# Silu on ScalarE in the shared MLP of a Mamba and mixture-of-experts layer

## What is computed

```python
xn = layernorm(x)
# mamba branch with a shared MLP behind it
h  = xn + mamba_mixer(rmsnorm(xn), ...)
s  = h + silu(rmsnorm(h) @ mlp_w1.T) @ mlp_w2.T      # 256 -> 1024 -> 256
# mixture of 8 experts, the 2 best of each token
g  = silu(moe(xn, ...))
out = x + s * g

def mamba_mixer(x, ...):                # 512 inner channels, 16 states
    xp, z = split(x @ in_proj_w.T)
    xc = silu(conv4(xp))
    dt = softplus(...); B, C = ...      # from xc @ x_proj_w.T
    state = state * exp(dt * A) + dt * xc * B        # a scan over the tokens
    y = sum_over_states(state * C) + xc * D
    return (y * silu(z)) @ out_proj_w.T
```

## The kernel before

| event | step in the period | what |
|---|---|---|
| A.IN0 to IN3, CV, TH, SL0 to SL3 | +15 to +39 | conv input, its taps on VectorE (L1395), tanh on ScalarE (L855), silu's multiplication on VectorE (L1405) |
| C.M100, M101, M102, M103 | +28, +31, +33, +35 | first MLP product for the first 256 tokens of the block, two of the eight 128-row groups in each |
| C.YE0, YE1 | +38 | the sum over states is taken in (L1420) |
| A.XD | +40 | x_proj on TensorE (L997, prod<-xc,par) |
| C.M200, M201 | +38, +40 | second MLP product of these tokens |
| C.Z0 | +41 | product for the gate z, tanh (L889), two multiplications on VectorE (L1426, L1434) |
| C.M110 to M113 | +43, +45, +47, +50 | first MLP product for the other 256 tokens |
| A.DT0 to DT3 | +44 to +50 | dt, Abs and Relu on ScalarE (L868, L869) |
| A.SPE, SPL | +51, +52 | softplus: Exp (L874), then Ln (L882); ScalarE comes to them 2 steps later by LATER |
| C.M210, M211, STORE | +53, +55, +57 | second MLP product, the block's result to DRAM (SP) |
| C.RMS, NORM | +17, +18 | Square (L894), Sqrt (L897), the norm's scaling (L901) |

## Time and profile before

### The profile page before, as it was taken

How to read it: one execution, slowest core, us unless ns; L and a number is a source line. 1 busy time by engine, 2 the same in 40 slices (tenths; PEclk the granted TensorE clock), 3 DMA queues, 4 the chain that set the end, 5 groups by cost and what they waited for, 6 DMA issues and landing times.

```text
span 1574.1 us, 17157 instructions
## 1 busy us (share of the span) xinstructions
PE 1273.4 (81%) x4966; PEld 922.0 (59%) x4966; DVE 1301.1 (83%) x1571; ACT 886.1 (56%) x1948; POOL 1197.2 (76%) x626
## 2 busy tenths in 40 slices
PE   3874563988979988988878997999978898889977
PEld 2641121765667747766756766775766576646546
DVE  6699875698879987999988986998889897977834
ACT  4642352584757656575757665775747374545532
POOL 0544888786898869887997779887988789896840
PEclk8586886899999979999989998999999998979989
DMA  4774443775496728685676748784868559455640
GB/s 165 263 268 146 161 147 106 267 256 175 144 317 208 244 89 268 232 259 164 201 250 231 221 145 274 227 246 148 256 224 251 181 172 302 140 191 188 211 152 27
DMA packets 129790, 319.50 MB, mean 203 GB/s; under 512 B 14984, under 2 KB 29712, under 8 KB 119200
## 3 DMA queue, kind: packets, MB, share of 16 engines
q1 hardware_dynamic: 112224, 272.91, 50.8%
q0 software_dynamic: 11328, 35.66, 9.5%
q10 hardware_dynamic: 6144, 9.83, 1.8%
HBM read 259.75 MB, written 39.71 MB: 190 GB/s over the span
## 4 chain that ended last, share of the span: by engine, by line
PE 28%; issue 22%; POOL 21%; DVE 11%; DMA 5%; ACT 4%; SPq 1%; DVEq 0%; ACTq 0%; POOLq 0%
PE prod L997 23%; POOL hxc L737 8%; DVE state L1382 7%; POOL dbu L726 7%; DMA xs<-slot_x 4%; POOL slot_x L713 3%; PE prod L1049 1%; PE prod L1184 1%; PE prod L1002 1%; PE prod L1185 1%; DVE hxc L1350 1%; ACT state L804 1%; POOL hxc L743 1%; DVE prod L1426 1%; DVE late L1452 1%
## 5 line engine op out<-in xcount | busy, mean ns | idle before, releaser
L1382 DVE TENSOR_TENSOR_SCAN state<-state,carry,dbu 128x512 f32<-128x512 f32 x512 | 657.1, 1283 | 117.3 <-ACT state L804 79.0
L726 POOL TENSOR_TENSOR dbu<-dtu,bb 128x1024 f32<-128x1024 f32 x256 | 624.9, 2444 | 52.8 <-DVE state L1382 45.9
L737 POOL TENSOR_TENSOR hxc<-hxc 128x1024 f32<-128x1024 f32 x155 | 370.2, 2388 | 176.1 <-DVE hxc L1350 176.1
L804 ACT ACTIVATE state<-dt,par 128x512 f32<-128x512 f32 x512 | 352.7, 692 | 73.9 <-DVE hxc L1350 58.8
L1350 DVE TENSOR_TENSOR hxc<-state,cb 128x512 f32<-128x512 f32 x512 | 353.4, 690 | 36.2 <-DVE state L1382 0.5
L997 PE MATMUL prod<-late 128*128 128x256 f32 x1136 | 276.0, 401 | 21.6 <-issue 20.9
L997 PE MATMUL prod<-xsT,late 128*128 128x256 f32 (+1 forms) x1280 | 269.7, 365 | 20.7 <-issue 8.8
L997 PEld LDWEIGHTS prod<-late 128*128 128x128 f32 x1136 | 233.3, 208 | 59.7 <-issue 32.0
L997 PEld LDWEIGHTS prod<-xsT,late 128*128 128x128 f32 x1280 | 225.5, 195 | 69.7 <-issue 32.3
L1049 PE MATMUL prod<-hxc,ident 128*128 128x512 f32 x212 | 123.4, 715 | 69.1 <-DVE hxc L1350 57.8
L802 ACT COPY carry<-state 128x1 f32<-128x1 f32 x384 | 61.0, 159 | 200.1 <-DVE hxc L1350 192.0
(11 more groups left out here) (166 smaller groups left out, 1318.4 us busy)
## 6 DMA issues: line engine op xcount, KB each, us to landing
bb<-bc_rows SPq DMA_DIRECT2D x256, 256.0 KB, 5.8
cb<-bc_rows SPq DMA_DIRECT2D x256, 256.0 KB, 4.8
late<-moe SPq DMA_DIRECT2D x40, 1028.0 KB, 5.1
late<-moe SPq DMA_DIRECT2D x40, 1024.0 KB, 6.3
hxc<-hxc POOLq DMA_DIRECT2D x36, 512.0 KB, 7.9
slot_x<-xc SPq DMA_DIRECT2D x18, 512.0 KB, 6.0
xs<-slot_x SPq DMA_DIRECT2D x31, 256.0 KB, 6.5
slot_y<-ys ACTq DMA_DIRECT2D x31, 256.0 KB, 5.2
```

What stands on the lines that cost most here:

```text
L726: nc.gpsimd.tensor_tensor(dbu[:, v % 3, :, :], dtu[:, n % 2, 2 * h:2 * h + 2, :], b, ALU.mult).then_inc(dbu_ready, 1)
L737: nc.gpsimd.tensor_tensor(hxc[:, to, :, :], hxc[:, to, :, :], hxc[:, piece, :, :], ALU.add).then_inc(summed, 1)
L804: nc.scalar.activation(state[:, k % STATES, :], dt[:, (2 * n + h) % 3, k % 2, :], ACT.Exp, scale=par[:, P_ALOG + col(k):P_ALOG + col(k) + ...
L1382: nc.vector.tensor_tensor_scan(state[:, k % STATES, :], state[:, k % STATES, :], dbu[:, v % 3, c, :], carry[:, n % 2, col(k):col(k) + 1], ...
```

## The change

ScalarE computes Silu of each first MLP product straight from the bank into `hid[:, 1]` and frees the bank; VectorE's multiplication goes away, with the semaphore `m_tanh` and the use of `th`. The factor 0.5 in the addition of M2 becomes 1.0. On ScalarE, the first event of each pair (M100, M102, M110, M112) is moved to the step of the second (SILU_PAIRS), so that both stand in the same step. The wait for the scatter of the routed rows (`scattered`, as `hid` lies over `xn_all`) moves from VectorE to ScalarE. Since ScalarE is now the reader of these banks, and at other steps, the planner gives out banks anew. TensorE's order is as before.

```diff
--- before.py
+++ after.py
@@ -89,7 +89,7 @@
 COST = {"UP": 4, "MT": 1, "DN": 9, "TR": 1, "IN": 4, "XD": 8, "DT": 2, "Z": 4, "OU": 8, "T1": 1,
         "M1": 4, "M2": 8}
 
-VECTOR_WORK = ("RO", "CV", "SL", "YE", "Z0", "Z1", "Z2", "Z3", "OU", "RC", "M1", "AD", "FI")
+VECTOR_WORK = ("RO", "CV", "SL", "YE", "Z0", "Z1", "Z2", "Z3", "OU", "RC", "AD", "FI")
 BETWEEN = ("CV", "YE", "OU", "M2")
 LATER = {"act": {"R": 1, "M": 1, "C": 1, "A": 2}, "dve": {"M": 1, "C": 1, "A": 0}, "pool": {"Y": 1, "A": 1},
          "pe": {"Y": 4}, "sp": {"M": 2}}
@@ -230,10 +230,17 @@
 EVENTS = events()
 
 
+SILU_PAIRS = {"M100": "M101", "M102": "M103", "M110": "M111", "M112": "M113"}
+
+
 def steps(engine):
 
     later = LATER.get(engine, {})
-    return [(k, e) for k, q, e in sorted((k + later.get(name[:2], later.get(kind, 0)), q, (kind, name, i))
+    def step(k, kind, name):
+        if engine == "act" and name in SILU_PAIRS:
+            k += STEPS_C[SILU_PAIRS[name]] - STEPS_C[name]
+        return k + later.get(name[:2], later.get(kind, 0))
+    return [(k, e) for k, q, e in sorted((step(k, kind, name), q, (kind, name, i))
                                          for q, (k, kind, name, i) in enumerate(EVENTS))]
 
 
@@ -250,7 +257,7 @@
         return "dve", (kind, "SL" + name[2], i)
     if kind == "C" and name[:2] == "M2":
         return "dve", (kind, "M2%s1" % name[2], i)
-    if kind == "C" and name[:2] != "T1":
+    if kind == "C" and name[:2] not in ("T1", "M1"):
         return "dve", (kind, name, i)
     if kind == "M" and name == "DN0":
         return "act", (kind, "DN%d" % (size(i) - 1), i)
@@ -308,7 +315,7 @@
 
 def tanh_order():
 
-    return [e for e in program("act") if e[0] == "C" and (e[1][0] == "Z" or e[1][:2] == "M1")]
+    return [e for e in program("act") if e[0] == "C" and e[1][0] == "Z"]
 
 
 USES = bank_uses()
@@ -461,7 +468,6 @@
         c_root = sem("c_root")
         c_inv = sem("c_inv")
         x1r_ready = sem("x1r_ready")
-        m_tanh = sem("m_tanh")
         s_out = sem("s_out")
 
         w1_in = sem("w1_in")
@@ -906,9 +912,12 @@
                         full(act, key)
                         nc.scalar.copy(x1T[:, int(name[2]), :], bank(key)).then_inc(*is_free(key))
                     elif name[:2] == "M1":
-                        tanh_free(act, key)
+                        q, pair = int(name[2]), int(name[3])
+                        if q == 0 and pair == 0:
+                            act.wait_ge(scattered, 16 * 2 * AT)
                         full(act, key)
-                        nc.scalar.activation(tanh_buffer(key), bank(key), ACT.Tanh, scale=0.5).then_inc(m_tanh, 1)
+                        nc.scalar.activation(hid[:, 1, 2 * pair:2 * pair + 2, :].rearrange("p r t -> p (r t)"), bank(key),
+                                             ACT.Silu).then_inc(*is_free(key))
                 elif kind == "L" and name == "ROOT":
                     act.wait_ge(stats, 2 * NORM_STEPS + 2 * (NB - 2))
                     nc.scalar.activation(roots[:, :, NT:], roots[:, :, NT:], ACT.Sqrt).then_inc(ln_root, 1)
@@ -1444,15 +1453,6 @@
                     elif name == "RCP":
                         dve.wait_ge(c_root, i + 1)
                         nc.vector.reciprocal(croot[:, :], croot[:, :]).then_inc(c_inv, 1)
-                    elif name[:2] == "M1":
-                        q, pair = int(name[2]), int(name[3])
-                        if q == 0 and pair == 0:
-                            dve.wait_ge(scattered, 16 * 2 * AT)
-                        dve.wait_ge(m_tanh, i * HC + q * (HC // 2) + pair + 1)
-                        nc.vector.scalar_tensor_tensor(
-                            out=hid[:, 1, 2 * pair:2 * pair + 2, :].rearrange("p r t -> p (r t)"),
-                            in0=tanh_buffer(key), scalar=1.0, in1=bank(key), op0=ALU.add, op1=ALU.mult
-                        ).then_inc(*is_free(key))
                     elif name[:2] == "M2":
                         if name[3] == "0":
                             return
@@ -1460,7 +1460,7 @@
                         key = (kind, "M2%d0" % q, i)
                         full(dve, key)
                         rows = x1[:, 2 * q:2 * q + 2, :]
-                        nc.vector.scalar_tensor_tensor(out=rows, in0=bank(key).rearrange("p (t d) -> p t d", t=2), scalar=0.5,
+                        nc.vector.scalar_tensor_tensor(out=rows, in0=bank(key).rearrange("p (t d) -> p t d", t=2), scalar=1.0,
                                                        in1=rows, op0=ALU.mult, op1=ALU.add).then_inc(*is_free(key))
                 elif kind == "D" and name[:2] == "AD":
                     b, q = i % 2, int(name[2])
```

## The result

| | before | after |
|---|---|---|
| median of 20 runs each | 1577.78 us (1568.35 to 1583.37) | 1583.92 us (1576.88 to 1590.17) |
| ratio | | 1.0037 (95%: 1.0023 to 1.0052) |
| profiled execution, span | 1574.1 us | 1579.2 us |

The change makes the kernel slower by 0.37%, 6 us. The forecast was 1586 us, +9 us.

What follows compares the result with a forecast made beforehand. No engine is full; VectorE sets time before XD, ScalarE at +56. Periods 3 to 6 add 8.4 us, periods 1 and 2 add 0.1 and 0.75: 9.25 on 1575.95, plus 1.1 to the median, 1586 us; range 1564 to 1602.

Steps and rivals of the forecast that it cites:

- group 4: M112/M113, on gapless ScalarE just before the +56 join: two loads and a moved activation add 3.1 us a period.
- VectorE loses 4.8 us a period: Eight removed multiplications (L1452) of 0.60 us per 64 scan steps, 2.4 before XD and 2.4 after Z0; waits counted nothing.
- 55 loads of 1283 ns, a pair for 2.6 us: On ScalarE, each silu pair between Exp decays needs two table loads; 55 more in all, 10.4 us a period.
- Rival 3: Each table switch costs a second wait as long as the load: 1602 us, chance 0.03.
- Groups 1 and 2: M100/M101 and M102/M103, ahead of XD: loads take 1.4 of 2.4 us saved, so -1.0 us a period.
- XD: TensorE product before Z0 at the +42 join; VectorE sets its start, expected about 1 us earlier in its period.
- Group 3: M110/M111, between Z0's tanh and +56: loads fit ScalarE's 4.9 us of waits, Z1's later tanh cancels the saving: 0.
- A shift at +56 is not swallowed: Delay where the scan waits for ScalarE passes through M210's addition, SP's store and expert-row loads to TensorE, uncompensated later.
- Rival 1: Loads hide in ScalarE's idle time around all four groups, making it faster, -14 or 15 us: 1562 us, chance 0.22.
- Rival 2: Everything sticks out; later evacuations and fuller banks hold TensorE at the joins: 5.6 us a period, 1611 us, chance 0.13.
- Period 7 and the tail: Group silus among gating silus in the last scan period, and the work after the scans: each set at 0.

Runs made afterwards that it cites:

- Run 1: Changed kernel with Tanh in place of Silu in the eight shared-MLP activations, so no added table loads: 1545.73 us, 0.9787 of the kernel before.
- run 2: Kernel before with silu on ScalarE only for M100 to M103, the first half of a block's tokens: 1569.63 us, ratio 0.9937.
- run 3: Kernel before with silu on ScalarE only for M112 and M113, M2 sums all taken by 0.5: 1583.03 us, ratio 1.0029.
- Run 6: Changed kernel with SILU_PAIRS empty, each silu at the step of its own product: 1599.72 us, 1.0146 of the kernel before.
- Run 8: Kernel before with silu on ScalarE for M100 to M103, M110 and M111, M112 and M113 left on tanh and VectorE: 1572.09 us, ratio 0.9978.

## Why the prediction was right, and where it was off

**Direction, size, mechanism: right.** +6 us measured, +9 forecast. Run 1 shows that the loads are the whole loss, run 2 that it comes from the second half of the block's groups, and run 3 that group 4 alone gives +11.2 of the 18.0 us there. The waits of VectorE from +52 to +58 grew by 3.9 us a period where 3 or more were expected; 1.2 of these also stand in run 1 without the loads. That the sum came so near has some luck in it: several terms below are off, and their errors cancel.

**VectorE loses 4.8 us a period.** Right: busy 43.3 us less for 64 instructions. Run 1 shows that all of it can reach the last scan, and more. The forecast had counted at nothing the time that VectorE waited for a tanh ahead of L1452, and that step is off: from period 1 to 7 these waits were 6.9 us, and without the loads VectorE's waits together went down by 8.0.

**55 loads of 1283 ns, a pair for 2.6 us.** Right, to the load. The load begins 0.02 us after the decay's end (1112.18 + 0.69, 1112.89), and its activation 0.02 us after the load's. Rival 3, a second wait as long as the load, falls: 3.10 us for a group hold no room for it. The Trainium skill (ScalarE: Activation LUTs, What ACT_TABLE_LOAD costs) states a drain of about 1380 ns at every switch beside the load; no load in the rows of after shows it. The same page of the Trainium skill has the rule, in section Table sets: the hidden batching unit, to batch calls by set. Run 6 agrees: the silus one by one, with 56 loads more, took 16 us more than in pairs.

**Groups 1 and 2: -1.0 us a period at XD.** Right in the mean: -6.7 us in six periods, -1.1 each, though single periods lie between -3.1 and +1.6. XD itself stands 0.6 us nearer to its period's start in the mean, between 3.2 nearer and 2.6 farther, where about 1 was expected. But two errors cancel here. Run 1 has -21.7 in this stretch, 3.6 a period: the 2.4 us of removed work and 1.2 us less waiting (28.3 us before, 21.0 in run 1, of all VectorE's waits in the stretch). So the loads of these two groups cost 2.5 us a period, where 1.4 were put down, and the saving was larger by as much.

**Group 3: 0.** Off in the sum. Run 8 against run 2 has +2.9 us for it in six periods. Together with group 4 it is more: after against run 2 has +21.3, and group 4 alone +11.2, so some 10 us come with group 3. By the table of periods 9.5 of the 10 fall in periods 1 and 2, and 0.5 in periods 3 to 6, where the forecast's 0 holds. The step that failed is that group 3 can be priced by itself, from the 4.9 us of idle time that one period showed. What the two groups share in periods 1 and 2 stays open: they may use the same idle time, but run 2 gained 6.6 us there for which the granted clock is a rival, and no run separates them.

**Group 4: +3.1 us.** The term itself is 3.10 us in the rows of period 5. Group 4 alone gives 2.6 to 3.0 in periods 3 to 6 (run 3). In periods 1 and 2 the forecast had ScalarE's waits for TensorE take up 2.01 and 1.35 us, which leaves 1.1 and 1.75; the table has +0.2 and +2.7 for the whole stretch. The sum of the two is right and each is off by 0.9. The clock that TensorE was granted there, 0.75 and 0.61 before and 0.94 and 0.78 after, was not in the forecast.

**A shift at +56 is not swallowed.** Off by the size. 4.2 us of the 18 come back between +56 and the next +28, up to 3.2 us in a period. One place can be seen in period 5. In before, the fifth scan behind that of 1114.92 waited 1.82 us for GpSimd. In after, the fifth scan behind that of 1127.37 is the one at 1137.80, and it waited for nothing. Timeline of VectorE, before, then after:

```profile
1127.25 1.29 DVE L1382 TENSOR_TENSOR_SCAN state<-state,carry,dbu 128x512 f32<-128x512 f32 x1 [1.82 <-POOL dbu L726]
```

```profile
1135.88 1.28 DVE L1391 TENSOR_TENSOR_SCAN state<-state,carry,dbu 128x512 f32<-128x512 f32 x1
1137.80 1.28 DVE L1391 TENSOR_TENSOR_SCAN state<-state,carry,dbu 128x512 f32<-128x512 f32 x1
```

A VectorE that comes later finds GpSimd's product done, and the lag of after falls there from 12.46 to 10.55 us (1135.88 against 1123.42, then 1137.80 against 1127.25). The forecast had followed the chain over SP and TensorE only. In period 2, 3.8 us more were lost in this stretch; what happened there I did not test.

**The sum.** Forecast: -6 + 0 + 15.25 + 0 = +9.25. Measured in the scans: -6.7 + 18.0 - 4.2 = +7.1, of which the profiled executions show 5.1 (they start 1.4 us apart) and the medians 6.1.

**Rivals.** Rival 1 (the loads hide) had the right potential and more: 32 us lie there, not 15, as run 1 shows. It fails as said, at group 4. Rival 2 (TensorE held by evacuations and banks) falls as far as banks and order go: the same ones without the loads give the best time of all. Period 7 and the tail, put at 0, came at -0.2 and -0.4.

## What to carry to other kernels

An activation of another table set costs its two loads wherever it stands, but they cost most where the engine that waits for ScalarE has no slack: find the stretch in which ScalarE shows no wait, and put no switch into it or just ahead of it. Of four equal pieces of such a change two paid and two did not; trying the halves separately turned a loss of 0.4% into a gain of 0.6%. Edits that each look free were not free together (2.9 and 11.2 us alone, 21.3 together), so measure them together before you call them free. And read the granted clock beside every stretch: where it differs between two runs, the difference of the stretch is not the price of the edit alone.

## What was not expected of the hardware

- Without the loads the scans gain more than VectorE's removed work: 34.0 us in six periods for 28.8 us of multiplications, with TensorE busy 1264 us of 1539 all the same. The rest is less waiting.
- TensorE's granted clock in the same five scans of a period (+46 to +51) differs between kernels that have the same work for it, from 0.61 to 1.00 in period 2, and the stretches move by some us with it.
- The price of a load falls with their number: 0.69 us each for the first 55, 0.28 for the next 56, at 1.28 us of ScalarE for every one.
